# A transformer block with mixture of experts: the keys' rotation made elementwise, and small VectorE instructions written as reductions

## The reference, cut to what matters

```
mod = silu(c) @ wmod                        # six rows per batch
h   = layernorm(x) * (1 + ca) + sa
q, k, v = rotate(rot[0], h), rotate(rot[1], h), rotate(rot[2], h)
#   rotate: pairs (even, odd feature), with c, s = rot pair / its norm:
#   y_even = c * x_even - s * x_odd ;  y_odd = c * x_odd + s * x_even
attn = softmax((2 + 2 * (q . k - 0)) / scale + bias) ;  ave = attn @ v
x   = x + ga * ave / sqrt(max(|ave|^2, 1e-8))
h   = layernorm(x) * (1 + cb) + sb
scores = softmax(h @ gate_w.T)              # 16 experts; each takes its 64 best tokens of a batch
out = shared feed-forward(h) + sum over experts of weight * feed-forward_e(h of its tokens)
x   = x + gb * out
```

## Time and profile before

| | |
|---|---|
| median of 3 runs | 2397.8 us (2396.78 to 2400.62) |
| profiled execution: its time, its span | 2398.3 us, 2396.5 us |
| PE busy | 2288.7 us (96%) |
| DVE busy | 1558.3 us (65%) |
| POOL busy | 1483.4 us (62%) |
| ACT busy | 1091.5 us (46%) |
| mean granted clock of TensorE | 0.988 |

### The profile page before, as it was taken

How to read it: one execution, slowest core, us unless ns; L and a number is a source line. 1 busy time by engine, 2 the same in 40 slices (tenths; PEclk the granted TensorE clock), 3 DMA queues, 4 the chain that set the end, 5 groups by cost and what they waited for, 6 DMA issues and landing times.

```text
span 2396.5 us, 40463 instructions
## 1 busy us (share of the span) xinstructions
PE 2288.7 (96%) x13620; PEld 1989.4 (83%) x13620; DVE 1558.3 (65%) x3098; ACT 1091.5 (46%) x2107; POOL 1483.4 (62%) x1253
## 2 busy tenths in 40 slices
PE   5999999999989999998989999999999999999997
PEld 4788888888878888787878888888888888888886
DVE  6777777887877888788766555455555554555543
ACT  4555665555645555564543333333333333333332
POOL 3566676666655666656555666666666666666664
PEclk8999999999999999999999999999999999999999
DMA  2212212211212121121243434444434444443433
GB/s 94 67 54 70 74 62 70 71 57 62 75 54 67 53 70 57 62 75 53 71 122 72 89 58 86 86 87 91 83 61 87 85 88 85 87 87 59 87 62 44
DMA packets 83002, 175.19 MB, mean 73 GB/s; under 512 B 12272, under 2 KB 47248, under 8 KB 82864
## 3 DMA queue, kind: packets, MB, share of 16 engines
q0 software_dynamic: 49152, 67.14, 17.5%
q1 hardware_dynamic: 33712, 106.05, 13.1%
HBM read 105.84 MB, written 67.31 MB: 72 GB/s over the span
## 4 chain that ended last, share of the span: by engine, by line
PE 69%; DVE 16%; issue 7%; ACT 4%; POOL 3%; DMA 0%; DVEq 0%; SPq 0%; ACTq 0%; POOLq 0%
PE ps L372 22%; PE ps L373 21%; PE ps L374 21%; PE ps L531 2%; DVE hidden_f L928 2%; DVE bn_stats L811 2%; ACT stage L668 1%; DVE neg_max L968 1%; DVE stage L912 1%; DVE stage L915 1%; DVE x_t L806 1%; ACT gelu L684 1%; DVE score_rows L1023 1%; PE ps L447 1%; POOL rstd L1204 1%
## 5 line engine op out<-in xcount | busy, mean ns | idle before, releaser
L372 PE MATMUL ps<-x_t,weights 128*128 128x512 f32 x1536 | 613.2, 399 | 41.8 <-DVE hidden_f L928 32.2
L1318 POOL DMA_INDIRECT out<-x_rows,step_token x256 | 417.9, 1632 | 308.9 <-DVE x_rows L1148 250.1
L373 PE MATMUL ps<-x_t,weights 128*128 128x512 f32 x1536 | 601.3, 391 | 0.0
L374 PE MATMUL ps<-x_t,weights 128*128 128x512 f32 x1536 | 599.6, 390 | 0.0
L372 PE MATMUL ps<-weights,hidden 128*128 128x256 f32 x2048 | 587.6, 287 | 10.0 <-POOL hidden L1208 4.9
L374 PE MATMUL ps<-weights,hidden 128*128 128x256 f32 x2048 | 581.6, 284 | 0.0
L373 PE MATMUL ps<-weights,hidden 128*128 128x256 f32 x2048 | 581.5, 284 | 0.0
L1171 DVE TENSOR_TENSOR hidden_f<-gelu,ps 128x512 f32<-128x512 f32 x256 | 175.6, 686 | 379.3 <-ACT gelu L786 325.4
L372 PEld LDWEIGHTS ps<-weights,hidden 128*128 128x128 f32 x2048 | 394.3, 193 | 19.3 <-issue 8.3
L373 PEld LDWEIGHTS ps<-weights,hidden 128*128 128x128 f32 x2048 | 394.5, 193 | 6.1
L786 ACT ACTIVATE gelu<-ps 128x512 f32<-128x512 f32 x256 | 152.4, 595 | 539.1 <-PE ps L374 522.8
(11 more groups left out here) (175 smaller groups left out, 3603.1 us busy)
## 6 DMA issues: line engine op xcount, KB each, us to landing
pairs<-mod_rows SPq DMA_DIRECT2D x36, 512.0 KB, 4.4
x_rows<-in_x SPq DMA_DIRECT2D x32, 512.0 KB, 3.5
h_rows<-stage SPq DMA_DIRECT2D x32, 512.0 KB, 2.6
out<-y_rows SPq DMA_DIRECT2D x32, 512.0 KB, 2.9
stage<-in_wg SPq DMA_DIRECT2D x16, 512.0 KB, 3.7
stage<-in_wd SPq DMA_DIRECT2D x16, 512.0 KB, 4.9
stage<-in_wu SPq DMA_DIRECT2D x16, 512.0 KB
mod_rows<-mod_rows SPq DMA_DIRECT2D x31, 256.0 KB, 3.2
```

What stands on the lines that cost most here:

```text
L372: pe.matmul(o, lhs(HI), rhs(HI), start=start, stop=False)
L373: pe.matmul(o, lhs(HI), rhs(LO), start=False, stop=False)
L374: return pe.matmul(o, lhs(LO), rhs(HI), start=False, stop=stop)
L1318: pool.indirect_dma_start(out=out_rows, out_offset=bass.IndirectOffsetOnAxis(ap=ICUR[g][:, t:t + 1], axis=0), in_=X1[:, g % 2, t * D:(t + ...
```

## The change

- **Transposes by even and odd features.** `x_transposes` reads every second feature (a step of two elements) instead of 128 neighbouring ones: half 0 of x_t holds the even features, half 1 the odd ones. A pair then lies in the same partition of both halves, and the rotation is R0 = c·x0 − s·x1, R1 = c·x1 + s·x0 with c and s per partition.
- **Keys without TensorE.** `keys` and its matrix are gone. ScalarE writes s times each half into `k_other` (new `KX`, beside each high copy in `h1_high`), VectorE's `keys_own` adds c times the other half and writes the keys into the PSUM banks where the matmuls left them, then `keys_high` (ScalarE) and `keys_low` (VectorE) split them. All this happens at the end of the stage before, behind `h1_low`, where it was at the start of the next one.
- **Order of selection.** `top_best` stays where it was, `top_strike` of the first round moves from before `hidden(i-1, 1)` to behind `keys_low`, except in stages that start a group. In stages 10, 18 and 26 the own part and the split of the keys stand behind `score_rows`.
- **Reductions.** The bias of the exponentials (was L973), `norm_squares` (was L934), the positions of the best (was L1028) and the collected scores (was L1003) are written as `tensor_reduce`. The first token of each batch is then added in `top_slots`, from a table that GpSimd fills once by 32 `memset`.
- **Setup.** The coefficients come from two transfers of 64 partitions, the swap matmul goes, and there are fewer setup instructions.

```diff
@@ TensorE
                 for k in range(KD):
                     for t in range(T):
-                        mm = pe.transpose(PC[:, k * S + t * P:k * S + (t + 1) * P], H1R[:, t, k * P:(k + 1) * P], IDENT)
+                        mm = pe.transpose(PC[:, k * S + t * P:k * S + (t + 1) * P],
+                                          H1R[:, t, :].rearrange("p (d j) -> p j d", j=2)[:, k, :], IDENT)
                     mm.then_inc(xt_done, 1)
-
-            def keys(n):
...
-                    mm = mm3(PC[:, (KD + k) * S:(KD + k + 1) * S], lambda a: ROTK[:, a, k, :],
-                             lambda a: H1_T[:, a, k, :], True, True)
-                    mm.then_inc(k_done, 1)
...
             def iteration(i, p, half, rounds=(), finish=None, start=None):
-                if valid(i):
-                    keys(i)
                 if valid(i - 2):
                     gate_up(i - 2, 3)
@@ ScalarE
+            def keys_high(n):
+                for k in range(KD):
+                    act.wait_ge(k_done, n * KD + k + 1)
+                    act.copy(K_T[:, HI, k, :], PC[:, (KD + k) * S:(KD + k + 1) * S]).then_inc(k_hi, 1)
+
             def h1_high(n):
+                if at(n, 0):
+                    act.wait_ge(rot_ready, 1)
+                wait(act, k_done, n * KD)
                 for k in range(KD):
                     act.wait_ge(xt_done, n * KD + k + 1)
+                    act.activation(KX[:, 1 - k, :], PC[:, k * S:(k + 1) * S], ACT.Copy,
+                                   scale=CS[:, 2 - k:3 - k]).then_inc(k_other, 1)
                     act.copy(H1_T[:, HI, k, :], PC[:, k * S:(k + 1) * S]).then_inc(h1_hi, 1)
...
                 if valid(i):
                     squares(i, (2, 3))
+                if valid(i + 1):
+                    keys_high(i + 1)
                 if valid(i - 1):
                     gelu(i - 1, 2)
@@ VectorE
+            def keys_own(n, k):
+
+                dve.wait_ge(k_other, (n + 1) * KD)
+                dve.wait_ge(h1_hi, n * KD + k + 1)
+                dve.scalar_tensor_tensor(PC[:, (KD + k) * S:(KD + k + 1) * S], PC[:, k * S:(k + 1) * S],
+                                         CS[:, 0:1], KX[:, k, :], ALU.mult, ALU.add).then_inc(k_done, 1)
+
+            def keys_low(n):
                 for k in range(KD):
-                    dve.wait_ge(h1_hi, n * KD + k + 1)
...
+                    dve.wait_ge(k_hi, n * KD + k + 1)
+                    split_lo(K_T[:, LO, k, :], PC[:, (KD + k) * S:(KD + k + 1) * S],
+                             K_T[:, HI, k, :]).then_inc(k_lo, 1)
...
-                dve.tensor_tensor(NSQ[:, :], ZZ[:, :], SSQ[:, :], ALU.max).then_inc(norm_sq, 1)
+                dve.tensor_reduce(NSQ[:, :], SQ_ZZ[:, :, :], AX.X, ALU.max).then_inc(norm_sq, 1)
...
-                dve.tensor_scalar(NB[:, both], NM[:, both], SCB[:, 5:6], SCB[:, 4:5], ALU.add,
-                                  ALU.add).then_inc(ebias, 2)
+                dve.tensor_reduce(NB[:, both], NM[:, both, :], AX.X, ALU.add).then_inc(ebias, 2)
...
-                dve.tensor_scalar(TOPI[:, :, bass.ds(r * 8, 8)], BESTU[:, :].unsqueeze(1).to_broadcast((P, 2, 8)),
-                                  CONST[:, bass.ds(g + C_BASE, 1)], None, ALU.add).then_inc(top_kept, 1)
+                dve.tensor_reduce(TOPI[:, :, bass.ds(r * 8, 8)],
+                                  BESTU[:, :].unsqueeze(1).to_broadcast((P, 2, 8)).unsqueeze(3), AX.X,
+                                  ALU.max).then_inc(top_kept, 1)
...
                     top_best(odd)
-                    top_strike(odd, g, r, before)
+                    if start is not None:
+                        top_strike(odd, g, r, before)
...
                 if valid(i - 1):
                     hidden(i - 1, 1)
+                apart = finish is not None or start is not None
                 if valid(i + 1):
-                    h1_low(i + 1)
+                    h1_low(i + 1, 0)
+                    if not apart:
+                        keys_own(i + 1, 0)
+                        keys_own(i + 1, 1)
+                    h1_low(i + 1, 1)
+                    if not apart:
+                        keys_low(i + 1)
+                for g, r, before in rounds[:1]:
+                    if start is None:
+                        top_strike(odd, g, r, before)
...
                 if start is not None:
                     score_rows(start, PC[:, 2 * S:3 * S])
+                if valid(i + 1) and apart:
+                    keys_own(i + 1, 0)
+                    keys_own(i + 1, 1)
+                    keys_low(i + 1)
                 if valid(i - 1):
                     hidden(i - 1, 2)
```

More of the change, by code:

```diff
@@ L139, in block_kernel @@
         IDX = sb("slot_token", [P, E, NG * TT], U32)
+        FIRST = sb("first_token", [P, NG * TT])
         WGT = sb("slot_weight", [P, E, NG * TT])
@@ L290, in _ @@
             sp.dma_start(CIN[:, :], c).then_inc(cond_in, 16)
-            sp.dma_start(ROT[:, :, :].rearrange("p a k -> p (a k)"), rot).then_inc(rot_in, 16)
+            for m in range(KD):
+                sp.dma_start(ROTR[m * (P // 2):(m + 1) * (P // 2), :],
+                             rot.rearrange("(j r) n -> j (r n)", r=2)).then_inc(rot_in, 16)
             sp.dma_start(X[:, 0, :], x_v[0]).then_inc(x_in[0], 16)
@@ L377, in _ @@
             pe.wait_ge(consts_in, 16)
-            pe.wait_ge(rot_in, 16)
-            pe.matmul(PG[:, 0:3 * KD], SWAP, ROT[:, :, :].rearrange("p a k -> p (a k)"),
-                      start=True, stop=True).then_inc(rot_sw_ps, 1)
             pe.wait_ge(silu_done, 1)
@@ L395, in rotation_rows @@
                 pe.wait_ge(rot_cols, 1)
-                for j, cols in ((0, COS[:, 2, :]), (1, CS[:, 3, :])):
-                    for k in range(KD):
-                        mm = pe.matmul(PG[:, j * D + k * P:j * D + (k + 1) * P], cols[:, k:k + 1].to_broadcast((P, P)),
-                                       IDENT, start=True, stop=True)
+                for j in range(2):
+                    mm = pe.matmul(PG[:, j * P:(j + 1) * P], ROT[:, 2, j:j + 1].to_broadcast((P, P)),
+                                   IDENT, start=True, stop=True)
                 mm.then_inc(rot_rows_ps, 1)
@@ L436, in scores @@
                         if t == 0:
+                            wait(pe, h1_hi, n * KD + k + 1)
+                            wait(pe, h1_lo, n * KD + k + 1)
                             wait(pe, k_hi, n * KD + k + 1)
@@ L707, in iteration @@
             def iteration(i, p, half):
-                if valid(i):
-                    for k in range(KD):
-                        act.wait_ge(k_done, i * KD + k + 1)
-                        act.copy(K_T[:, HI, k, :], PC[:, (KD + k) * S:(KD + k + 1) * S]).then_inc(k_hi, 1)
                 if valid(i - 2):
@@ L868, in rotations @@
-                link(dve.tensor_copy(ROTK[:, HI, :, :], ROTF[:, :, :]))
-                split_lo(ROTK[:, LO, :, :], ROTF[:, :, :], ROTK[:, HI, :, :]).then_inc(rot_ready, 1)
+                dve.tensor_copy(NM[:, :, 1], ncz.to_broadcast((P, T)))
+                link(dve.tensor_copy(NM[:, :, 2], cz.to_broadcast((P, T))))
+                qc, qs, kc, ks = (ROT[:, a, j:j + 1] for a in range(2) for j in range(2))
+                link(dve.tensor_tensor(CS[:, 0:1], qc, kc, ALU.mult))
+                link(dve.tensor_tensor(CS[:, 3:4], qs, ks, ALU.mult))
@@ L1035, in top_slots @@
                     rows = slice(h * CAP, (h + 1) * CAP)
-                    for o, dst in ((0, IDX), (P, WGT)):
-                        last = dve.tensor_copy(
-                            dst[rows, :, bass.ds(g * TT, TT)],
-                            ps[rows, o:o + P].rearrange("p (q h e) -> p h e q", h=2, e=E)[:, h])
+                    slots = (ps[rows, o:o + P].rearrange("p (q h e) -> p h e q", h=2, e=E)[:, h] for o in (0, P))
+                    dve.tensor_tensor(IDX[rows, :, bass.ds(g * TT, TT)], next(slots),
+                                      FIRST[rows, bass.ds(g * TT, TT)].unsqueeze(1).to_broadcast((CAP, E, TT)), ALU.add)
+                    last = dve.tensor_copy(WGT[rows, :, bass.ds(g * TT, TT)], next(slots))
                 last.then_inc(tops_read, 1)
@@ L1193, in _ @@
         def _(pool):
+            for q in range(NG * TT):
+                for h in range(2):
+                    last = pool.memset(FIRST[h * CAP:(h + 1) * CAP, q:q + 1], float((2 * q + h) * S))
+            last.then_inc(first_set, 1)
+            pool.wait_ge(first_set, 1)
             pool.wait_ge(consts_in, 16)
```

109 lines of the change are left out of this document (47 added, 62 removed).

## The result

| | before | after |
|---|---|---|
| median | 2397.7 us (2396.78 to 2400.62) | 2434.4 us (2433.84 to 2434.68) |
| profiled execution: time, span | 2398.3, 2396.5 us | 2434.6, 2432.8 us |
| mean granted clock | 0.988 | 0.969 |

The ratio is 1.0149, with a 95% interval of 1.0137 to 1.0161: slower by 1.5%. The direction was forecast, the size was not: 2434.4 us lies above the range of 2384 to 2428.

A forecast was written before the change was run, and what follows sets the result against it. TensorE's own matmul list was taken as the bound, with gelu and product setting each tail. Stage terms of -3.7 us and +16 us for clock drops gave +12.3 us on 2398.3: 2410.6 us, range 2384 to 2428.

The forecast's parts named there:

- filling of the pipeline: Kernel start: earlier keys let batch 0's scores start about 3 us sooner; -3.8 us, between 0 and -6.
- 8 stages without selection: Stages 2 to 9: the keys' 1.39 us of matmuls go, but gelu and product still set the tail; gain 0.
- stage 10, with clock: VectorE makes own and low parts after `score_rows`, before the product: +2.0 us, plus one clock drop of 1.6 us.
- 14 one-round stages, without clock: Stall before `gate_up(·, 2)` goes, 2.75 us idle arises before `gate_up(·, 3)`; -0.24 us a stage, -3.4 us in all.
- stage 18: New work hides in TensorE's 7.39 us idle for no semaphore, and the keys' matmuls go: -1.7 us.
- stage 26, with clock: VectorE's new parts delay the product, the reduction shortens the way to `score_rows`: +1.2 us, plus a 1.6 us clock drop.
- two-round stages, with clock: Stages 27 to 30: two strikes and `top_best` precede the product; 38.87 against 38.37 us, +2.0 us, plus four clock drops.
- the clock's part: TensorE's clock falls after long idle pieces: ten drops of 1.6 us, +16 us; rivals: clock holds (0.25), all 14 drop.
- the 0.2 charged for `ln2_centre`: Behind the bias, `ln2_centre` meets the rest of `v_sum` and `v_sum` starts later: 0.2 us per stage.
- 0.28 us for a restart: One-round stages: this restart cost was to go along with the 1.44 us stall before `gate_up(·, 2)`.
- All six long pieces: Idle pieces of about 5 us in stages 10, 26 and 27 to 30, each counted as a 1.6 us clock drop.
- Strided transposes at double cost: Rival, chance 0.07: transposes with a step cost double, +1 us in 31 stages, 2441 us.

The follow-up runs named there:

- the fill: Changed kernel plus matmuls in the tail whose results nobody reads (6, and 18 in the lists from stage 28 on): 2406.0 us, ratio 1.0024 to the kernel before.
- strike early: Changed kernel with the first round's strike back before `hidden(i-1, 1)`: 2435.9 us, ratio 1.0143 to the kernel before.
- keys only: Changed kernel with the four reductions put back to the instructions of before: 2442.4 us, ratio 1.0175 to the kernel before.
- fill of three: Changed kernel with 3 matmuls in every tail whose results nobody reads: 2417.4 us, ratio 1.0059 to the kernel before.
- strike late: Changed kernel with the one-round strike, and the second of two rounds, behind the next stage's `attention_out`: 2383.9 us, ratio 0.9932 to the kernel before.
- reductions only: Kernel before with just the four reductions and the table of first tokens: 2359.7 us, ratio 0.9827 to the kernel before.
- loop written out: Kernel of reductions only with the loop over the first two selection groups unrolled: 2349.5 us, ratio 0.9786 to the kernel before.

## Why the prediction was right in direction and wrong in size

Measured terms are differences of stages between the two profiled executions, rounded; the sum is that of the executions. The clock's share of the one-round stages is what the fill took away.

| term | forecast | measured |
|---|---|---|
| filling of the pipeline | -3.8 | -1.5 |
| 8 stages without selection | 0 | +1.0 |
| stage 10, with clock | +3.6 | +2.1 |
| 14 one-round stages, without clock | -3.4 | +2.7 |
| 14 one-round stages, clock | +6.4 (4 drops) | +20.2 (14 drops) |
| stage 18 | -1.7 | -3.4 |
| stage 26, with clock | +2.8 | +3.6 |
| two-round stages, with clock | +8.4 | +10.2 |
| the rest | 0 | +1.5 |
| sum | +12.3 | +36.3 |

**The step that failed** is the one in the clock's part: "Whether a piece of 2.75 us is followed by the low clock I can't tell from one row: between none and all of 14. I take four". All 14 were. The piece was forecast at 2.75 us and came at 2.8 to 2.9; its price, 1.6 us, measured 1.44 (38.45 in the changed kernel less 37.01 with the fill), as a mean of four falls at 1.97 and ten at 1.23. Ten more falls at this price are 14.4 us, and the lower price of the four takes 0.6 off: 13.8 of the 24 us that were missing. The one row near it, 2.78 us at 1207.58, pointed that way, and I gave it too little weight; four was a guess between none and 14. The text itself had all 14 at 2426.6 us, inside its range; it is the second miss and smaller ones that carry the time past 2428. How steady this is the other runs tell: in strike early (2.62 to 2.81 us) it was all 14 again, in keys only 9 of 14, with a fill of three (1.96 to 2.23 us) 7, in the fill and in strike late (1.28 to 1.54 us) none. So a count between none and 14 was possible. The changed kernel's four executions lie within 0.9 us, less than one fall, which speaks for all 14 in each of them.

**The second miss** is the one-round tail with the clock held: 37.0 us a stage instead of 36.6 (36.37 and the 0.2 charged for `ln2_centre`), 6.1 us over 14 stages. The idle time is as forecast plus 0.1 us. The rest was taken from a stage without selection. But TensorE's busy time beside the keys was already 247.51 / 7 - 1.39 = 33.97 us in a one-round stage before, and 280.38 / 8 - 1.39 = 33.66 us in one without selection; in reductions only, where the stall is gone, it is 245.17 / 7 - 1.39 = 33.63 us. The extra 0.3 us went with the stall. I had counted it as gone ("0.28 us for a restart"), but a stall remained, only in another place: (248.77 / 7) - 1.38 of fill = 34.16 us in the run with the fill. The remaining 0.1 to 0.2 us are in stages without selection, too (35.25 for 35.12). The eight strided transposes last 1.20 us in the stage shown, and 1.16 on average over these stages,

```profile
332.69 1.20 PE L417 MATMUL ps<-consts,stage 128*128 128x128 f32 x8
```

where they took 1.06 and 1.05 on average. That is about the growth; the transposes were not tested by themselves.

**What held.** The keys' matmuls were worth nothing where there is no selection: 9.85 us of work gone, 1.0 us more time, and in reductions only they are all there in stages as short. The tail is set by gelu and product. The strike went from one wait into another, and the first of the two is one that the reductions alone remove. All six long pieces had the low clock behind them, as forecast, though that of stage 10 was 2.80 us and not about 5. A two-round stage with the clock held takes 39.03 us in the fill, for 38.87 forecast. Strided transposes at double cost, a rival, would be 1 us a stage; it is 0.1. The rule of the page "SBUF — State Buffer" of the Trainium skill, section "SBUF: two separate sides", by which GpSimd and a VectorE instruction with two SBUF inputs shut each other out for whole instructions, was the ground for expecting that the bias's wait would be passed on. The trace agrees: 844 to 159 ns there, 478 to 732 ns behind it. In size, VectorE's keys took 0.75 us for one and 1.41 for two, inside 0.5 to 0.9, and a scaled copy 0.68 us instead of about 0.5.

**What the prediction did not ask** is what each part does alone. It charged the reductions with a gain only beside the moved strike (-0.44 us a stage); in the old order the same four lines bring 1.73 us a stage. The elementwise keys, with their transposes and setup, cost 76 us in the old order beside the reductions (strike early less reductions only), and moving the strike behind them won none of it back.

**Open.** What beside its length decides on the clock after an idle piece of 2 to 3 us: the changed kernel and strike early had it low after all 28, keys only after 9 of 14 of 2.66 to 2.98 us. That wasn't taken apart. Nor was what makes one fall cost 1.23 and another 1.97 us; two-round falls cost 1.9. How the 0.3 us of a stalled one-round stage arise, and whether the fill adds to them. Which of the four reductions brings the 1.73 us: that it is the positions of the best, 2.13 us in the way of the product, is read from the earlier trace rows and from its 0.23 us in keys only; the four were never tested apart.

## What to carry to other kernels

Before work is taken off an engine, look whether it lies in a wait that stays: a stage without selection took 35.1 us with these matmuls and 35.25 without, and in a longer wait work in their place kept the engine's clock up. Whoever moves work to another engine should look what now stands ahead of the instruction that frees a buffer, and time each half of a change alone, for here one half gave -1.7%, and the other took that and 1.5% more. Where one row has a price and a pattern repeats 14 times, take the row's case for all 14, and keep the other as a rival, with a range that holds both.

## What the runs showed of the hardware

- In the one-round stages of the runs, idle pieces of TensorE of 1.28 to 1.54 us were never followed by the low clock (before, fill, strike late), those of 1.96 to 2.23 us in 7 of 14 cases, those of 2.62 to 2.98 us in 37 of 42. A fall costs 1.2 to 2.0 us beside the idle time, and matmuls in the gap whose results nobody reads gave it back (28 us in all). Length is no sure sign at the other end either: at the start of phase B of the fastest run (loop written out) a piece of 1.61 us was followed by matmuls of 256 columns at 0.41 instead of 0.28 us; the pieces of 1.70 to 1.90 us of the kernel before had none behind them.
- A VectorE `tensor_scalar` beside a GpSimd instruction on SBUF took 2.13 us for 16 numbers per partition and 1.34 us for 2; as `tensor_reduce` they took 0.17 and 0.16 us. With no GpSimd instruction beside it the one of 16 took 0.23 us as it was.
- At the jump back over a long loop body TensorE stood 7.39 us (before) and 5.57 us (reductions only) for no semaphore, with the low clock behind; written out, 1.27 us were left, which waited for real work.
